# Sorting edges by source: 240 of 800 columns scattered by GpSimd, 560 placed by TensorE

## Time and profile before

| | |
|---|---|
| median of 3 runs | 7416.21 us (7399.02 to 7418.02) |
| the execution with the profile | 7403.44 us, its span 7401.6 us |
| PE busy | 4706.3 us (64%) |
| DVE busy | 4623.4 us (62%) |
| POOL busy | 4497.2 us (61%) |
| ACT busy | 2409.1 us (33%) |
| mean granted TensorE clock | 0.786 of 2.4 GHz |

### The profile page before, as it was taken

The page is one execution under the profiler, slowest core; times in us unless marked ns, Lnnn a source line. Parts: engine busy times, 40 slices in busy tenths (PEclk is TensorE's granted clock), DMA queues, the critical chain, the costliest instruction groups (busy, mean ns, idle before and its releaser), DMA issues.

```text
span 7401.6 us, 95264 instructions
## 1 busy us (share of the span) xinstructions
PE 4706.3 (64%) x19009; PEld 2793.2 (38%) x19009; DVE 4623.4 (62%) x10963; ACT 2409.1 (33%) x5954; POOL 4497.2 (61%) x4196
## 2 busy tenths in 40 slices
PE   6599822223388887526676667666665766666588
PEld 2255411111244444314444436333333633333365
DVE  7877755555566667626666655666665566666553
ACT  0188700000166663014444442222221222222131
POOL 0000177777677778877777762777776277777600
PEclk9899955555599998758888878777776877777789
DMA  4000177777665553236666682666667376766700
GB/s 111 18 0 0 35 227 224 228 226 231 176 152 152 152 152 73 57 95 211 210 209 210 210 174 94 208 211 212 211 208 174 95 211 211 211 208 210 174 26 18
DMA packets 506841, 1150.06 MB, mean 155 GB/s; under 512 B 115695, under 2 KB 244306, under 8 KB 506497
## 3 DMA queue, kind: packets, MB, share of 16 engines
q0 software_dynamic: 187648, 458.07, 24.6%
q1 hardware_dynamic: 271844, 551.41, 22.5%
q10 hardware_dynamic: 47136, 138.12, 6.6%
HBM read 864.81 MB, written 281.13 MB: 155 GB/s over the span
## 4 chain that ended last, share of the span: by engine, by line
POOL 40%; issue 21%; PE 7%; DMA 4%; DVE 1%; POOLq 0%; ACT 0%; SPq 0%; DVEq 0%; ACTq 0%
POOL sort_mem L540 26%; POOL recB_d L513 14%; DMA sort_mem<-x_d,x_mem 4%; PE banks L1144 4%; PE banks L1039 1%; PE banks L1049 1%; PE banks L1134 1%; DVE xnt_mem L1345 0%; PE banks L1107 0%; POOLq L537 0%; POOL acc_mem L523 0%; DVE z_mem L1689 0%; POOL acc_mem L498 0%; DMA x_mem<-recB_d 0%; POOLq L119 0%
## 5 line engine op out<-in xcount | busy, mean ns | idle before, releaser
L540 POOL DMA_INDIRECT sort_mem<-x_d,x_mem x2568 | 2636.8, 1027 | 838.6 <-issue 796.9
L1107 PE MATMUL banks<-z_mem 128*128 128x257 f32 x5136 | 2065.4, 544 | 1192.6 <-DVE acc_mem L1507 1072.4
L1107 PEld LDWEIGHTS banks<-z_mem 128*128 128x128 f32 x5136 | 1168.8, 257 | 2075.8 <-DVE acc_mem L1507 1475.9
L1507 DVE TENSOR_TENSOR acc_mem<-acc_mem,banks 128x257 f32 x3376 | 1420.8, 421 | 528.5 <-PE banks L1107 162.5
L779 ACT ACTIVATE z_mem<-z_mem 128x512 f32<-128x512 f32 x1284 | 790.3, 631 | 2388.8 <-DVE z_mem L1689 2388.7
L498 POOL DMA_INDIRECT acc_mem<-h_d,z_mem x808 | 813.7, 1007 | 1135.5 <-ACTq L631 890.9
L1689 DVE TENSOR_TENSOR z_mem<-x_mem,sort_mem 128x512 f32<-128x512 f32 x1284 | 833.2, 691 | 961.3 <-DMA sort_mem<-x_d,x_mem 955.2
L513 POOL DMA_INDIRECT recB_d<-sort_mem x800 | 1010.5, 1263 | 270.5 <-issue 270.5
L954 PE MATMUL banks<-ident,z_mem 128*128 128x128 f32 x808 | 225.1, 434 | 728.0 <-DVE z_mem L1446 728.0
L1005 PE MATMUL banks<-acc_mem,z_mem 128*128 128x257 f32 x1616 | 545.5, 420 | 143.2 <-DVE acc_mem L1507 123.1
L937 PE MATMUL banks<-xnt_mem,acc_mem 125*128 125x512 f16 (+1 forms) x3200 | 549.2, 335 | 0.0
(11 more groups left out here) (274 smaller groups left out, 4786.6 us busy)
## 6 DMA issues: line engine op xcount, KB each, us to landing
x_mem<-ew_d SPq DMA_DIRECT2D x428, 512.0 KB, 4.2
ew_d<-x_mem SPq DMA_DIRECT2D x214, 512.0 KB, 3.0
pay_d<-acc_mem SPq DMA_DIRECT2D x202, 516.0 KB, 4.3
acc_mem<-pay_d ACTq DMA_DIRECT2D x202, 516.0 KB
x_mem<-recB_d SPq DMA_DIRECT2D x642, 68.0 KB
sort_mem<-x_d,x_mem POOLq DMA_INDIRECT x2568
edge_d<-xnt_mem ACTq DMA_DIRECT2D x40, 332.0 KB
sort_mem<-edge_d SPq DMA_DIRECT2D x40, 332.0 KB
```

The source lines that it names most:

```text
L540: pool.indirect_dma_start(out=xg[h % XG][:, k, :], out_offset=None, in_=x_d, in_offset=bass.IndirectOffsetOnAxis(ap=reci[h][:, k, W_SRC:W_ ...
L1107: m.matmul(bank[5 + tile % 3][:, :AC], oneh[:, Q % 2, k, :], msg[:, Q % 2, k, :], start=True, stop=True)\
L1507: v.tensor_tensor(a_, a_, bank_[:, :AC], ALU.add).then_inc(flushed, 1)
```

## The change

`SENT` is 240 and `PUT` 560. The first 240 columns of sort A are no longer placed by PE.

- SP clears a new DRAM table `recA_d` of 128 x 808 records of two numbers, ahead of the fills of `recB_d`.
- In `split_slots` DVE makes the record address `row * 808 + tile` of 240 columns (`sent_at`) and copies their two values side by side (`sent`), then signals `sent_ready`.
- POOL waits for that and for all fills, and issues 240 indirect DMAs of 125 records of 8 B. They count on the semaphores `edges_put0` to `3`, whose later waits are raised by 960 (`SENT * 4`). From the 80th on, every 20 wait for those issued 80 earlier.
- SP, after the store of `h` and when all 240 have landed, reads the table back to `sent_back` in SBUF (827 KB) and adds 16 to `h_stored`.
- The loops of the put on DVE, ACT and PE run over the other 560 columns.
- DVE waits for `h_stored` at 32 and adds `sent_back` as it copies the banks to `recA`.
- A semaphore is renamed (`acc_half` into `acc_zeroed`), and one that nobody waited for goes.

```diff
--- before.py
+++ after.py
@@ -42,6 +42,9 @@
 XG = 4
 EW = 4
 LAG = 5
+SENT = 240
+assert SENT % 80 == 0
+PUT = EC - SENT
 assert TB // 4 % TURN == 6
 assert TA // 4 == EC // 4 + 2
 W_SRC, W_SEG = 32, 33
@@ -178,6 +181,9 @@
         pick = acc_mem[:EP, o:o + 80].bitcast(BF16); o += 80
         lone = acc_mem[:EP, o:o + 2 * 256].bitcast(FP16).rearrange("p (h k s) -> p h k s", h=2, k=4); o += 2 * 256
         lput = acc_mem[:EP, o:o + 2 * 512].bitcast(FP16).rearrange("p (h k v s) -> p h k v s", h=2, k=4, v=2); o += 2 * 512
+        sent = acc_mem[:EP, o:o + 2 * SENT].rearrange("p (c v) -> p c v", v=2); o += 2 * SENT
+        sent_at = acc_mem[:EP, o:o + SENT].bitcast(INT32); o += SENT
+        sent_back = acc_mem[:, o:o + 2 * TA].rearrange("p (t c) -> p t c", c=2); o += 2 * TA
         acc_end = (BKT_B + 1) * AC
         assert o <= acc_end, o
 
@@ -287,6 +293,7 @@
 
 
         recB_d = dram("recB_d", [P * TB, RW])
+        recA_d = dram("recA_d", [P * TA, 2])
         edge_d = dram("edge_d", [EP, EC * RW])
         h_d = dram("h_d", [NP_, HC])
         pay_d = dram("pay_d", [P, TA * HC])
@@ -329,6 +336,9 @@
                     .then_inc(S("att_w_loaded"), 16)
 
             sp.wait_ge(S("fill_ready"), 1)
+            sp.dma_start(recA_d.rearrange("(p a t) c -> p a (t c)", p=P, a=4),
+                         zeros[:, :TA // 2].rearrange("p (a c) -> p a c", a=1).broadcast_to([P, 4, TA // 2]))\
+                .then_inc(S("filled"), 16)
             rows8 = recB_d.rearrange("(p q t) c -> p q (t c)", p=P, t=8)
             for q in range(0, TB // 8, 27):
                 n = min(27, TB // 8 - q)
@@ -337,6 +347,11 @@
 
             sp.wait_ge(S("htab_ready"), 1)
             sp.dma_start(h_d.rearrange("(t p) c -> p t c", p=P), htab).then_inc(S("h_stored"), 16)
+
+            sp.wait_ge(S("h_stored"), 16)
+            for u in range(4):
+                sp.wait_ge(S(f"edges_put{u}"), SENT * 4)
+            sp.dma_start(sent_back, recA_d.rearrange("(p t) c -> p t c", p=P)).then_inc(S("h_stored"), 16)
 
             def keep(i, quads=10):
                 for j in range(quads):
@@ -354,7 +369,7 @@
             def stage_edges(n):
                 for u in range(4):
                     if due(n * 320):
-                        sp.wait_ge(S(f"edges_put{u}"), n * 320)
+                        sp.wait_ge(S(f"edges_put{u}"), n * 320 + SENT * 4)
                         sp.sem_inc(S("passed"), 1)
                     i = 4 * n + u
                     sp.dma_start(stB[:EP, u, :, :].rearrange("p c w -> p (c w)"),
@@ -483,6 +498,16 @@
             pool.wait_ge(S("p_const"), 12)
             pool.sem_inc(S("fill_ready"), 1)
 
+            pool.wait_ge(S("sent_ready"), 1)
+            pool.wait_ge(S("filled"), 16 * (1 + -(-(TB // 8) // 27)))
+            for c in range(SENT):
+                u = c // 20 % 4
+                if c >= 80 and c % 20 == 0:
+                    pool.wait_ge(S(f"edges_put{u}"), c // 80 * 320)
+                pool.indirect_dma_start(
+                    out=recA_d, out_offset=bass.IndirectOffsetOnAxis(ap=sent_at[:, c:c + 1], axis=0),
+                    in_=sent[:, c, :], in_offset=None).then_inc(S(f"edges_put{u}"), 16)
+
             def gather_h(i, quads=10):
                 for j in range(quads):
                     h, turn, Q = j % 5, 2 * i + j // 5, 10 * i + j
@@ -513,17 +538,16 @@
                         pool.indirect_dma_start(
                             out=recB_d, out_offset=bass.IndirectOffsetOnAxis(ap=stB_i[:EP, u, k:k + 1], axis=0),
                             in_=stB[:EP, u, k, :], in_offset=None).then_inc(S(f"edges_put{u}"), 16)
-            pool.wait_ge(S("filled"), 16 * (-(-(TB // 8) // 27)))
             looped(pool, BODIES // 4, scatter_edges)
             for l in range(LAYERS):
                 if l == 0:
                     pool.wait_ge(S("x2_ready"), 1)
                     for u in range(4):
-                        pool.wait_ge(S(f"edges_put{u}"), BODIES // 4 * 320)
+                        pool.wait_ge(S(f"edges_put{u}"), BODIES // 4 * 320 + SENT * 4)
                     g.memset(acc_mem, 0.0).then_inc(S("acc_zeroed"), 1)
                 if l:
                     pool.wait_ge(S("flat_ready"), (l - 1) * NT + NT)
-                    g.memset(acc_mem[:, 0:38 * AC], 0.0).then_inc(S("acc_half"), 1)
+                    g.memset(acc_mem[:, 0:38 * AC], 0.0).then_inc(S("acc_zeroed"), 1)
 
                 pool.wait_ge(S("state_stored"), l * 80 + 80)
                 pool.wait_ge(S("x2_moved"), 16)
@@ -609,14 +633,14 @@
                 if due(4 * Q - 4):
                     act.wait_ge(S("column_put"), 4 * Q - 4)
                 for k in range(4):
-                    c = ds(4 * Q + k, 1)
+                    c = ds(4 * Q + k + SENT, 1)
                     a.activation(lput[:, h, k, 0, :], lone[:, h, k, :], ACT.Copy, scale=dstm[:, c]).then_inc(S("values_put"), 1)
                     a.activation(lput[:, h, k, 1, :], lone[:, h, k, :], ACT.Copy, scale=segp[:, c]).then_inc(S("values_put"), 1)
 
             def put_pair(i):
                 for h in range(2):
                     put_values(2 * i + h, h)
-            looped(act, EC // 8, put_pair)
+            looped(act, PUT // 8, put_pair)
 
             def stage_quad(Q, h, turn):
                 if due(Q - 4):
@@ -939,11 +963,11 @@
                     last.then_inc(S("column_put"), 1)
             put_columns(0, 0, first=True)
             put_columns(1, 1)
-            with pe.Fori(1, EC // 8 - 1) as i:
+            with pe.Fori(1, PUT // 8 - 1) as i:
                 for h in range(2):
                     put_columns(2 * i + h, h)
-            put_columns(EC // 4 - 2, 0)
-            put_columns(EC // 4 - 1, 1, final=True)
+            put_columns(PUT // 4 - 2, 0)
+            put_columns(PUT // 4 - 1, 1, final=True)
             pe.wait_ge(S("recA_made"), 4)
 
             def turn_v(Q, h):
@@ -1194,7 +1218,6 @@
             st.did(v.scalar_tensor_tensor(keyB, rel_i, float(NT), hi_i, ALU.mult, ALU.add))
             st.did(v.tensor_copy(itemB[:, 1, :], lo_i))
             st.settle()
-            dve.sem_inc(S("items_ready"), 1)
 
             def count(s):
                 nb, cols, n_, T = s["nb"], s["cols"], s["n"], s["T"]
@@ -1290,6 +1313,10 @@
                 st.run(v.tensor_copy(hi_i, slotf))
                 st.run(v.tensor_single_scalar(lo_i, hi_i, 127, ALU.bitwise_and))
                 st.run(v.tensor_single_scalar(hi_i, hi_i, 7, ALU.logical_shift_right))
+                st.did(v.scalar_tensor_tensor(sent_at, lo_i[:, :SENT], float(TA), hi_i[:, :SENT], ALU.mult, ALU.add))
+                st.did(v.tensor_copy(sent[:, :, 0], dstm[:, :SENT]))
+                st.run(v.tensor_copy(sent[:, :, 1], segp[:, :SENT]))
+                dve.sem_inc(S("sent_ready"), 1)
                 st.did(v.tensor_copy(loA, lo_i))
                 st.run(v.tensor_copy(tileA, hi_i))
 
@@ -1399,21 +1426,23 @@
                 if due(4 * Q - 4):
                     dve.wait_ge(S("column_put"), 4 * Q - 4)
                 v.tensor_tensor(lone[:, h, :, :], iota_b[:EP].rearrange("p (a s) -> p a s", a=1).broadcast_to([EP, 4, P]),
-                                loA[:, ds(4 * Q, 4)].rearrange("p (c a) -> p c a", a=1).broadcast_to([EP, 4, P]),
+                                loA[:, ds(4 * Q + SENT, 4)].rearrange("p (c a) -> p c a", a=1).broadcast_to([EP, 4, P]),
                                 ALU.is_equal).then_inc(S("lo_ready"), 1)
                 for k in range(4):
-                    v.tensor_scalar(tone[:, h, k, :], iota_h[:EP], tileA[:, ds(4 * Q + k, 1)], None, ALU.is_equal)\
+                    v.tensor_scalar(tone[:, h, k, :], iota_h[:EP], tileA[:, ds(4 * Q + k + SENT, 1)], None, ALU.is_equal)\
                         .then_inc(S("tiles_hot"), 1)
 
             def hot_pair(i):
                 for h in range(2):
                     hot_columns(2 * i + h, h)
-            looped(dve, EC // 8, hot_pair)
-            dve.wait_ge(S("column_put"), EC)
+            looped(dve, PUT // 8, hot_pair)
+            dve.wait_ge(S("column_put"), PUT)
+            dve.wait_ge(S("h_stored"), 32)
             for c, add in ((0, float(MID)), (1, -1.0)):
                 for b in range(2):
                     n = min(512, TA - 512 * b)
-                    v.tensor_scalar(recA[:, 512 * b:512 * b + n, c], bank[2 * c + b][:, :n], add, None, ALU.add)\
+                    v.scalar_tensor_tensor(recA[:, 512 * b:512 * b + n, c], bank[2 * c + b][:, :n], add,
+                                           sent_back[:, 512 * b:512 * b + n, c], ALU.add, ALU.add)\
                         .then_inc(S("recA_made"), 1)
             dve.wait_ge(S("recA_made"), 4)
 
@@ -1661,7 +1690,7 @@
                 if l:
                     dve.wait_ge(S("flat_ready"), (l - 1) * NT + NT)
                     st.did(v.memset(acc_mem[:, 38 * AC:], 0.0))
-                    dve.wait_ge(S("acc_half"), l - 1 + 1)
+                    dve.wait_ge(S("acc_zeroed"), l + 1)
```

## The result

| | before | changed |
|---|---|---|
| median of 4 runs | 7417.11 us (7399.02 to 7418.45) | 7254.57 us (7243.5 to 7259.57) |
| ratio | | 0.9784, 95% interval 0.9771 to 0.9797 |
| the execution with the profile | 7403.4 us | 7243.5 us, its span 7241.5 |

The forecast was 7248 us and, from the profiled execution, 7241.4. Some executions take some 15% longer (one of the four with 160 columns took 8537 us, and on one occasion all did, the kernel before 8510 us), and every ratio here compares executions of one level alone.

The account below looks back on a forecast made before the run. The put was taken as bound by TensorE and on the path with its full length. Terms -164.8 + 1.0 + 1.8 = -162.0 gave 7241.4 us from the profile, 7254.2 from the median; 7248 was named, range 7228 to 7325.

Parts of the forecast that it names:

- Removed from TensorE: In the put, TensorE places 240 fewer columns at 0.6865 us each: -164.8 us, while it stays the bound.
- Added to DVE: Ahead of the layer norm, three new instructions over 240 columns at 0.35 us each: +1.0 us.
- DVE beside scatters in the head: In the head's layer norm, seven scatters hold VectorE's L1345 products by 0.26 us each: +1.8 us.
- POOL in the head: From 253 us to the put's start at 340.5, 57 scatters at pitch 1.48 us, with 2 us of delays.
- POOL beside the put: During the put, the remaining 183 scatters at pitch 1.70 us end at 652, hidden behind its end at 727.
- The read back: After POOL's last scatter, landing and reading back 0.8 MB take 7 us, hidden before the put's end.
- The end of the put: The four L1416 combining instructions, 2.03 us, become two-source at the same length: 0 added.
- The sum: Over the whole kernel, -164.8 + 1.0 + 1.8 = -162.0 us, giving 7241.4 us from the profiled 7403.4.
- One scatter a quad: Rival, chance 0.26: DVE's chain per four put columns holds POOL, 43 scatters follow the put; +71 us, 7318.
- POOL stands still: Rival, chance 0.05: no scatter gets done in the put, all 183 and the read follow, 278 us; 7526.
- DVE pays: Rival, chance 0.04: each scatter holds the put's DVE for its whole 1.18 us; +137 us, 7385.

Follow-up runs that it names:

- the run with late scatters: Changed kernel, but POOL waits for the end of the head (`htab_ready`) before its first scatter: 7239.7 us, ratio 0.9784.
- unused ones: Changed kernel with 240 columns scattered and read back, but TensorE places all 800 and nothing is added: 7401.1 us, ratio 1.0011.
- the two-source kernel: Changed kernel with the put's `tone` compare made a two-source `tensor_tensor`: 7442.2 us, run once.

## Why the prediction was right

The forecast came out in its steps, and nearly in its numbers.

- *Removed from TensorE*, -164.8: the put took 385.6 us where it took 549.2, -163.6. A column cost 0.6886 instead of 0.6865 us, and without scatters it was 0.6879, so most of this is not the scatters: about 2 us of the put don't shrink with its columns.
- *Added to DVE*, +1.0: 0.94 us.
- *DVE beside scatters in the head*, +1.8: +1.2 in the layer norm, and gone when no scatter runs there. The put started 2.0 us later than before, where 2.8 were due, but that this is so near is partly luck: it is 1.0 less because the head ran earlier up to L1315, 0.98 and 1.17 more by the two terms, and 0.8 more in the projection, which the run with late scatters has as well, and the runs without scatters and with unused ones have not.
- *POOL in the head*, 57 scatters at 1.48: 59 start there, (341.6 - 252.3) / 1.49 = 60 at the free pitch. The first takes 1.55 us and the one beside the first `a1` product (L1404) 2.02, where I had allowed 2 us of delays for such products in all.
- *POOL beside the put*, pitch 1.70: this is the term that was off, to the good. (624.4 - 341.6) / 181 = 1.56, 0.08 over 1.48 and not 0.22. (The expectations written behind it say 1.545, because I divided by the 183 of the forecast; 181 started beside the put.) I had added 0.07 for L1401 and 0.15 for L1405. Measured, a scatter that starts while DVE idles takes 1.19 us on average, one that starts in a compare 1.25, and one that starts in L1428 1.33: over the 181 that makes 0.03 for L1428 and 0.04 for the compares. POOL ended at 624, not 652. It changed no time, because POOL has 100 us to spare; with 280 columns it is what leaves 7 us of room (699.7 - 685.5 - 6.9), where a pitch of 1.70 would have used them up and cost 24: 221 scatters beside the put x 0.14 = 31.
- *The read back*, 7 us, hidden: 6.9 from the last scatter's start in the run with 320, and hidden here.
- *The end of the put*: the four combining instructions take 2.03 us as before, and the first gather is 4.9 us behind PE's last column in both.
- The sum, -162.0: the span is 160.1 shorter, the medians 162.5. That all terms came within 1.3 us is the account; that the two sums lie within 2 us of -162.0 is luck as well, since single stages behind the put differ by up to 7 us between executions.

The rivals. *One scatter a quad* (7318) would have left scatters behind the put; the last was 103 us ahead of it, and 181 fell in the first 103 of 140 quads ((624.4 - 341.6) / 2.75), 1.8 each. *POOL stands still* (7526) falls with the same row. *DVE pays* (7385): DVE's waits fell from 0.70 us a quad (137.5 / 197) to 0.57 (78.3 / 138), which is 138 x 0.13 / 181 = 0.10 us a scatter and not 1.18, and the idle time takes it up.

I gave one scatter a quad 0.26 because of the earlier trace rows, and there the reason that I gave for preferring was wrong: a number of sources doesn't tell the two apart, as the two-source kernel shows. The Trainium skill, "SBUF — State Buffer", section "SBUF: two separate sides", has the pair of ports as an exclusive lock: who starts first keeps it for the whole instruction, and the other fully blocks. By that rule, if it covers these compares, the scatter at 501.40, 1.20 us beside four such compares, should have waited up to 0.4 us for its start, and a compare should have waited 1.2 us for it. This trace agrees only in that a start can be late by part of one instruction (1.18 to 1.44 us beside the put, 1.53 beside two-source compares), not that either engine stands still for the other's length: the longest compare was held by 0.3 us. Nor do the rows that I set against the page and for it bear on such an instruction: L1345 is f32 and takes 256 elements in 0.33 us, fewer than one a nanosecond where L1405 does more than two, and L1301 has two sources. Of the compares, only the bf16 ones hold POOL for their whole chain.

## What to carry to other kernels

Where one engine is alone on the path and another idles through the same stretch, divide the items between them and work out where both end together: here 0.69 us a column against 1.56 us a scatter plus 7 us for the read back, which meet near 283 of 800, and 280 was the best of four splits. Read the pitch of the second engine from rows beside the very instructions that it will meet, not from their kind; an indirect DMA was held 0.06 us on average by one kind of compare and up to 1.5 us (2.45 against 0.95) by another. Where an engine that issues indirect DMAs binds a stage, look for its longest instruction: one kind of chain, of four compares, taken apart gave 26 us.

## What the runs showed of the hardware

- Four bf16 compares of 125 x 375 in a row hold an indirect DMA to their end (2.45 us instead of 0.95), four f16 compares of 125 x 808 with one source or two, and eight of 125 x 404 with two, do not (1.18 to 1.53 instead of 1.19). One bf16 compare by itself holds it by 0.4 us at most (1.34 instead of 0.95). What makes the difference (the type, the broadcast operand, the table that is read, or that the first are gathers and the others scatters) was not tried apart.
- Four one-source f16 compares are in turn held by scatters, each by 0.3 us at most (0.72 us instead of 0.42).
- A scatter of 125 records costs POOL the same with 8 B a record (1.18 to 1.19 us and 0.30 between) as with 136 B.
- A chain of 25 products in the layer norm takes 1.2 us more with some six scatters beside it, 0.2 each.
- In executions in which the kernel before takes 8510 us, 240 scatters, 181 of them beside the put, stretch it by 51 us (600.2 instead of 549.2); in those of 7400 us by nothing.
